# First layer's state space kernel: the near waves multiplied on GpSimd, in quarters

## What is computed

```python
dtA = dt[:, None] * A
dC = C * (jnp.exp(dtA) - 1.0) / A
powers = jnp.exp(dtA[:, :, None] * jnp.arange(L))
K = 2.0 * jnp.einsum('dn,dnl->dl', dC, powers).real
```

## Time and profile before

| | us |
|---|---|
| median of 3 runs | 670.03 (669.6 to 674.61) |
| profiled execution, its own time | 671.23 |
| its span, first to last instruction | 669.4 |
| busy in the span: PE, PEld | 492.3, 357.1 |
| DVE, ACT, POOL | 438.0, 258.7, 207.8 |
| mean granted TensorE clock | 0.851 of full speed |

### The profile page before, as it was taken

The page is one execution under the profiler, slowest core; times in us unless marked ns, Lnnn a source line. Parts: engine busy times, 40 slices in busy tenths (PEclk is TensorE's granted clock), DMA queues, the critical chain, the costliest instruction groups (busy, mean ns, idle before and its releaser), DMA issues. The chain is left out here.

```text
span 669.4 us, 11535 instructions
## 1 busy us (share of the span) xinstructions
PE 492.3 (74%) x4041; PEld 357.1 (53%) x4041; DVE 438.0 (65%) x1422; ACT 258.7 (39%) x625; POOL 207.8 (31%) x245
## 2 busy tenths in 40 slices
PE   4597537473599776987768577978598889899960
PEld 2265423361577555776645466756277646455530
DVE  4569896999844777655574998895678554133225
ACT  4499702120013433654113636452266232133321
POOL 3224000553723002655010532330374037044440
PEclk9679955777899886998987677989889879999995
DMA  8100006010000031660000000000735001500012
GB/s 277 43 3 2 1 0 252 9 26 2 0 1 1 0 83 41 114 142 1 1 0 1 2 1 1 1 1 2 290 144 134 2 5 55 138 28 32 29 39 91
DMA packets 28195, 33.44 MB, mean 50 GB/s; under 512 B 5176, under 2 KB 21288, under 8 KB 27625
## 3 DMA queue, kind: packets, MB, share of 16 engines
q1 hardware_dynamic: 26204, 29.24, 14.9%
q0 software_dynamic: 1504, 3.15, 1.4%
q10 hardware_dynamic: 432, 0.33, 0.2%
HBM read 26.50 MB, written 6.21 MB: 49 GB/s over the span
## 5 line engine op out<-in xcount | busy, mean ns | idle before, releaser
L3305 DVE TENSOR_TENSOR em_inner<-banks,em_soft 128x256 f32<-128x256 f32 x31 | 13.1, 424 | 52.5 <-ACT em_soft L3141 52.5
L1777 POOL TENSOR_TENSOR ea_scaled_rows<-ea_scaled_rows 128x768 f32<-128x768 f32 (+2 forms) x24 | 27.7, 1155 | 61.6 <-ACT ea_scaled_rows L1704 60.3
L3189 POOL DMA_INDIRECT em_results<-em_y_slot,slot_rows x31 | 29.7, 957 | 49.7 <-DVE em_y_slot L3313 48.8
L219 ACT ACTIVATE norm_log<-norm_var 128x4 f32<-128x4 f32 x20 | 4.1, 205 | 85.6 <-DVE norm_var L197 85.5
L3079 PE MATMUL banks<-em_up,em_slotT 128*128 x62 | 34.9, 645 | 0.0
L1704 ACT ACTIVATE ea_scaled_rows<-banks,ea_gate 128x192 f32<-128x192 f32 x64 | 23.4, 419 | 25.5 <-PE banks L38 25.4
L2343 POOL TENSOR_TENSOR ga_to_end<-ga_cum 128x512 f32<-128x512 f32 x8 | 12.4, 1545 | 65.1 <-DVE ga_cum L2399 65.0
L1207 POOL TENSOR_TENSOR xa_prob<-xa_score,xa_top 128x308 f32<-128x308 f32 x8 | 5.6, 703 | 75.9 <-DVE xa_left L1304 75.9
L3141 ACT ACTIVATE em_soft<-banks 128x256 f32<-128x256 f32 x31 | 11.9, 383 | 42.7 <-PE banks L3079 42.7
L579 POOL TENSOR_TENSOR lin_q_strip<-lin_qT,lin_strip_head 128x512 f32<-128x512 f32 x8 | 13.9, 1741 | 43.6 <-PE banks L461 29.9
L2738 POOL TENSOR_TENSOR ca_prob<-ca_prob,ca_most 128x1232 f32<-128x1232 f32 x8 | 18.0, 2247 | 19.6 <-DVE ca_most L2791 19.6
(11 more groups left out here) (508 smaller groups left out, 1543.3 us busy)
## 6 DMA issues: line engine op xcount, KB each, us to landing
em_up<-in_em_up SPq DMA_DIRECT2D x3, 1536.0 KB, 11.3
ea_wide<-ea_gates SPq DMA_DIRECT2D x4, 1024.0 KB, 17.0
em_down<-in_em_down SPq DMA_DIRECT2D x3, 768.0 KB, 12.7
em_slots<-slot_rows SPq DMA_DIRECT2D x1, 2108.0 KB, 11.2
w_qkv<-in_w_qkv SPq DMA_DIRECT2D x1, 1536.0 KB, 7.7
slot_rows<-em_slots SPq DMA_DIRECT2D x1, 1360.0 KB, 8.1
cos_lag<-in_cos_lag SPq DMA_DIRECT2D x1, 1024.0 KB, 5.7
sin_lag<-in_sin_lag SPq DMA_DIRECT2D x1, 1024.0 KB, 8.0
```

The costliest lines, as they stand in the source:

```text
L1777: step(pool.tensor_tensor(scaled_rows[:, k, 0:n], scaled_rows[:, k, 0:n], scaled_rows[:, k, n:2 * n], ALU.add))
L3189: pool.indirect_dma_start(core.results[:, :], bass.IndirectOffsetOnAxis(ap=slot_rows[:, s, P:P + 1].bitcast(U32), axis=0), y_slot[:, s % N ...
```

## The change

GpSimd does `near_product`, at the end of its list, in quarters of 32 channels: eight multiplications, four sums, four products of 128 x 512. VectorE's steps at g = 5 and 6 are gone. A semaphore `weights_ready` tells GpSimd that the weights are written; `near_done` now counts to 4. The two semaphores of the pads become one.

```diff
--- before.py
+++ after.py
@@ -401,7 +401,7 @@
         running = core.bank[BANKS - 1][:, 0:2 * P]
         scored = core.banks[:, 0:STRIPS, :].rearrange("p r (j t) -> p r j t", j=SH)
 
-        pads_zeroed, ones_ready = sem("pads_zeroed"), sem("ones_ready")
+        pads_ready = sem("pads_ready")
         elu_exp = sem("elu_exp")
         k_rows_relu = sem("k_rows_relu")
         elu_done = sem("elu_done")
@@ -466,7 +466,7 @@
                     s.claim(pe)
                     first, last = g % HT == 0, g % HT == HT - 1
                     if g == 0:
-                        pe.wait_ge(ones_ready, 3)
+                        pe.wait_ge(pads_ready, 5)
                     pe.wait_ge(v_ready, g // 2 + 1)
                     ring[f"ks{g // HT}{g % HT // 2}"].taken(pe)
                     pe.wait_ge(elu_done, 4 * (g // HT) + 4)
@@ -535,7 +535,7 @@
                         else:
                             ins.then_inc(k_rows_relu, 1)
 
-                            act.wait_ge(pads_zeroed, 2)
+                            act.wait_ge(pads_ready, 2)
                             g = HT * b + 2 * (int(name[3]))
                             for i in range(2):
                                 ins = act.copy(v_diagonal(g + i),
@@ -564,13 +564,14 @@
 
             @block.gpsimd
             def _(pool):
+                step = core.steps(pool, "pool")
                 kernel.constants(pool)
-                pool.memset(v_pad[:, :, :, :], 0.0).then_inc(pads_zeroed, 1)
-                pool.memset(one_pad[:, :], 0.0).then_inc(pads_zeroed, 1)
-                pool.wait_ge(pads_zeroed, 2)
-                pool.memset(diagonal(one_pad[:, :]), 1.0).then_inc(ones_ready, 1)
-                pool.memset(ones[:, :], 1.0).then_inc(ones_ready, 1)
-                pool.memset(tiny[:, :], 1e-6).then_inc(ones_ready, 1)
+                pool.memset(v_pad[:, :, :, :], 0.0).then_inc(pads_ready, 1)
+                pool.memset(one_pad[:, :], 0.0).then_inc(pads_ready, 1)
+                pool.wait_ge(pads_ready, 2)
+                pool.memset(diagonal(one_pad[:, :]), 1.0).then_inc(pads_ready, 1)
+                pool.memset(ones[:, :], 1.0).then_inc(pads_ready, 1)
+                pool.memset(tiny[:, :], 1e-6).then_inc(pads_ready, 1)
                 pool.wait_ge(heads_ready, 1)
                 for g in range(NT):
                     pool.wait_ge(elu_done, 4 * (g // HT) + 1)
@@ -578,6 +579,8 @@
                         pool.wait_ge(scores_ready, STRIPS * (g - 1))
                     pool.tensor_tensor(q_strip[:, g % 2], spread(qT[:, g], 1, [P, SH, P]),
                                        spread(strip_head[:, :], 2, [P, SH, P]), ALU.mult).then_inc(strip_ready, 1)
+                kernel.near_product(pool, step)
+                core.keep("pool", step)
 
             @block.vector
             def _(dve):
@@ -647,8 +650,6 @@
                         kernel.fraction(dve, "near", g - 1)
                     elif g in (3, 4):
                         kernel.fraction(dve, "far", g - 3)
-                    elif g in (5, 6):
-                        kernel.near_product(dve, step, g - 5)
                     elif g == 7:
                         for n in range(2):
                             kernel.far_product(dve, n)
@@ -713,6 +714,7 @@
         self.fractions = {"near": sem("near_fraction"), "far": sem("far_fraction")}
         self.sines = {"near": sem("near_sines"), "far": sem("far_sines")}
         self.near_sizes, self.far_sizes = sem("near_sizes"), sem("far_sizes")
+        self.weights_ready = sem("weights_ready")
         self.near_done, self.far_done = core.sem("near_done"), core.sem("far_done")
         self.taps_out, self.taps_in = core.sem("taps_out"), core.sem("taps_in")
 
@@ -829,24 +831,31 @@
         step(dve.tensor_tensor(cm, nr, are, ALU.mult))
         step(dve.tensor_tensor(q, ni, aim, ALU.mult))
         step(dve.tensor_tensor(cm, cm, q, ALU.add))
-        step(dve.scalar_tensor_tensor(cm, cm, 2.0, re, ALU.mult, ALU.mult))
+        dve.scalar_tensor_tensor(cm, cm, 2.0, re, ALU.mult, ALU.mult).then_inc(self.weights_ready, 1)
         step(dve.tensor_tensor(em, ni, are, ALU.mult))
         step(dve.tensor_tensor(q, nr, aim, ALU.mult))
         step(dve.tensor_tensor(em, em, q, ALU.subtract))
-        step(dve.scalar_tensor_tensor(em, em, 2.0, re, ALU.mult, ALU.mult))
-
-    def near_product(self, dve, step, n):
-
-        shape = [P, P, LB]
-        w = [x[:, :, :] for x in self.wave]
-        if n == 0:
-            dve.wait_ge(self.sines["near"], 2)
-            step.mark(dve.tensor_tensor(w[0], w[0], spread(self.small[5][:, :], 2, shape), ALU.mult))
-            step(dve.tensor_tensor(w[1], w[1], spread(self.small[4][:, :], 2, shape), ALU.mult))
-        else:
-            step(dve.tensor_tensor(w[0], w[0], w[1], ALU.add))
-            dve.wait_ge(self.near_sizes, LB)
-            dve.tensor_tensor(self.near[:, :, :], w[0], self.near[:, :, :], ALU.mult).then_inc(self.near_done, 1)
+        dve.scalar_tensor_tensor(em, em, 2.0, re, ALU.mult, ALU.mult).then_inc(self.weights_ready, 1)
+        dve.wait_ge(self.weights_ready, 2)
+
+    def near_product(self, pool, step):
+
+        parts = [slice(32 * j, 32 * j + 32) for j in range(4)]
+        shape = [P, 32, LB]
+        pool.wait_ge(self.weights_ready, 2)
+        pool.wait_ge(self.sines["near"], 2)
+        for d in parts:
+            for n, weight in enumerate((self.small[5], self.small[4])):
+                w = self.wave[n][:, d]
+                step.mark(pool.tensor_tensor(w, w, spread(weight[:, d], 2, shape), ALU.mult))
+        step.wait()
+        for d in parts:
+            w = [x[:, d] for x in self.wave]
+            step.mark(pool.tensor_tensor(w[0], w[0], w[1], ALU.add))
+        step.wait()
+        pool.wait_ge(self.near_sizes, LB)
+        for d in parts:
+            pool.tensor_tensor(self.near[:, d], self.wave[0][:, d], self.near[:, d], ALU.mult).then_inc(self.near_done, 1)
 
     def far_product(self, dve, n):
         dve.wait_ge(self.sines["far"], n + 1)
@@ -858,7 +867,7 @@
     def multiply(self, pe, slot):
 
         slot.claim(pe)
-        pe.wait_ge(self.near_done, 1)
+        pe.wait_ge(self.near_done, 4)
         pe.wait_ge(self.far_done, 2)
         for d in range(P // 4):
             for j in range(4):
```

## The result

| | before | changed |
|---|---|---|
| median of 20 runs each, us | 672.62 (669.6 to 675.22) | 675.26 (673.87 to 677.59) |
| profiled execution, us | 671.23 | 676.77 |
| its span, us | 669.4 | 675.0 |

The ratio is 1.0044, 95% interval [1.0029, 1.0059]: the changed kernel is 3.0 us slower, and the interval leaves 2 to 4 us. (The ratio is an estimate of its own, not the quotient of the two medians, which differ by 2.6 us.

A forecast was written before the change was run, and what follows sets the result against it. VectorE looked like the bound in the first layer's stretch (busy 7.83 of 8.00 us). Gain 1.4 and loss 5.3 make +3.9 us, from the median 670.03 to 673.9; own range 672.5 to 675.5, whole range 668.5 to 678.0.

The forecast's parts named there:

- GpSimd's list: First layer's block: sixteen GpSimd operations, multiplications 1.04 us, sums and products 1.27, ending at 86.9; no bound as such.
- The rival by L2343's 1.545: GpSimd's broadcast multiplications and the rest cost 1.545 us each; block 7.8 us late, 677.8 us; chance 12%.
- The first two passes: Two VectorE passes ahead of the first norm: removing them gains nothing, since the norm waits for ScalarE's root until 80.25.
- 1.4 us from the second two: Two VectorE passes ahead of gather 7's division: removing them gains 1.4 us, then TensorE is late next.
- Turns: First norm behind the root: VectorE and GpSimd alternate one instruction each, putting L622 at 87.2 instead of 81.90.
- only some are held: Rival in the first norm: L203 but not four-element instructions held, or four L203 pass together; 672.8 us or less; 22%.
- they slip in between: Rival: the norm's short VectorE instructions pass between GpSimd's operations, norm ends at 81.98, 1.4 us gained, 668.6 us; 13%.
- The size of the delay: State pass L622 after the first norm comes 5.3 us late; bounds 0 and 9.2 us.
- Behind the norm: Gather 7 at 94.2, division 7 3.9 us later; rest of block and following layers follow one for one.
- Edits at nothing: Merged pad semaphore and weight writes near 17 us: one wait lost, under 0.1 us, and a wait on themselves gained.

The follow-up runs named there:

- the second comparison: The changed kernel and the kernel before, both unaltered, run and profiled again: ratio 1.0080 [1.0049, 1.0111], medians 677.16 against 672.57 us.
- multiplications only: Changed kernel with GpSimd's four sums and four products left out and done by nobody: ratio 0.9999 [0.9967, 1.0031] to the kernel before.
- whole tiles: Changed kernel with GpSimd's passes as four instructions over 128x2048 instead of quarters: ratio 1.0047 [1.0020, 1.0075] to the kernel before.

## Why the prediction was right

It said +3.9 us, and the runs say +3.0 (2 to 4), in the second comparison +5.4 (3.3 to 7.5; the medians differ by 4.6); what both intervals hold is 3.3 to 4.0. The blocks themselves show +3.15 and +3.35. The time itself, 673.9, was built on three runs with a median of 670.03, and the kernel before stands at 672.62 over twenty; that 675.26 still fell into the forecast's own range, 672.5 to 675.5, is in part luck, since the base lay 2.6 us too low and the rise was put 0.9 us too high. Step by step:

- **GpSimd's list.** Forecast: eight at 1.04, eight at 1.27, 17.5 us from the end of the first (69.4) to the end of the last (86.9). Measured: 1.02, 1.24 and 1.23, 17.2 us from 70.25 to 87.47. The rival by L2343's 1.545 falls: that operand's repetition costs nothing, a multiplication with it is the cheaper form.
- **The first two passes are worth nothing.** Held: with the norm's variance ready at 74.4 the idle entry ahead of L199 grew (7.22 us, with a root 1.3 late), and the kernel that gives sum and product back to VectorE has net 0.0.
- **1.4 us from the second two.** Held: -1.34 counted from the root's end and -1.47 from the span's start in multiplications only, with the wait for TensorE that was named.
- **Turns.** Held, with the four-element instructions included; "only some are held" and "they slip in between" fall by L201's 1.11 us here and by L199's 4.20 us in whole tiles. What the forecast didn't have is the gap between sums and products, in which one instruction (L200 here, L201 in the second profile) goes free.
- **The size of the delay** is the term that was mis-sized. Forecast 5.3 us (L622 6.95 behind the root), measured 4.5 and 4.7 (6.16 and 6.36). The forecast let GpSimd finish third sum, fourth sum and four products at a distance of 1.3 to 1.4 us, adding VectorE's own pieces to GpSimd's durations. They aren't added: the products, with a VectorE instruction let in at each, stand 4.93 / 4 = 1.23 us apart, the sums, mostly without, 1.24. From the end of the fourth sum to the end of the products the forecast had 5.3 us, both profiles have 5.0. The other part is where the root met the list: 1.55 us ahead of the end of the fourth sum in the forecast, 0.89 in the first profile, where GpSimd began without a hold and the third sum was already done, and 1.34 in the second.
- **Behind the norm** everything followed one for one, as said: net is delay less 1.35 in every such profile.
- **Edits at nothing**: the wait that the weights lose is seen near 17 us: from the reciprocal's start to the end of the weights it is 3.59 us before and 3.47 with the change, 0.12 us less, where under 0.1 was said. GpSimd's five memsets end at 5.76 us in both kernels. None of these edits was tried alone.

What stays open is why the second comparison gives 5.4 us where the block accounts for 3.2 to 3.4. The intervals allow both to be 3.3, and the four profiles (568.6 and 569.4 us behind the next layer's start, 569.8 and 569.2 with the change) show no cost in the later layers beyond the spread of 1 us.

## What to carry to other kernels

Before work is moved to GpSimd, list the VectorE instructions that will run while it runs there. Here those with two inputs in SBUF (L199 to L201) and the tensor_scalar ones (L197, L203) were held, and statistics and instructions with one operand in PSUM were not. Each of the first kind may pay one whole two-input GpSimd instruction, however small it is itself, and if they stand on the critical path the delay is about the number of turns times GpSimd's duration, at most until its list is empty, less what the move uncovers. Moved to where no instruction of the path is held by it, and taken from where VectorE really is the bound, the work is worth nearly its full VectorE time: here 2.2 us of 2.28 by the profiles, after the norm had been drawn forward. And read the duration of tiny instructions in the timeline: a hold shows there as busy time, not as idle time, and no share of the span will tell of it.

## What the runs showed of the hardware

- A one-input GpSimd instruction (tensor_scalar, 128x512, 1.47 us) held VectorE's norm instructions only for about its first 0.6 us (one profile), a two-input one (1.23 us) until its end. The slower instruction was the better neighbour: 0.95 us lost instead of 4.5. The Trainium skill (SBUF — State Buffer, Who interferes with whom) lets a VectorE instruction with two inputs in SBUF contend with any GpSimd instruction that reads SBUF, and names no difference between GpSimd's forms. L201's 0.62 us beside an instruction that ran 1.47, and L199's and L200's 0.16 beside the one before, disagree with a hold to the end for this form.
- A gap of 0.07 to 0.08 us between GpSimd instructions, from a wait on its own semaphore, lets a VectorE instruction of 0.16 us through: L200 at 82.52, L201 at 79.78 and at 77.37 in three profiles.
- On GpSimd an instruction over 128x2048 takes 4.49 us where four over 128x512 take 4.93 and eight over 128x256 5.51; the multiplications by a repeated weight take 7.33, 8.19 and 9.31 us for both waves.
- The end of ScalarE's root moved between 78.39 and 81.80 us over executions of the same two kernels, by as much as the effect that was studied. TensorE's L445 took 3.78 us at a granted clock of 0.50 in three of these profiles and 1.98 at 1.00 in the fourth, the one with the earliest root. Only times counted from a common event could be compared.
